# Rotary attention: probabilities times values as three fp16 passes, and slots of TensorE, VectorE and ScalarE in another order

## The reference

```python
def _L3_attn_ref(x, w_qkv, w_out):          # H = 16 heads, D = 128
    qkv = jnp.einsum('bsd,od->bso', x, w_qkv).reshape(B, S, 3 * H, D)
    q, k, v = qkv[:, :, :H, :], qkv[:, :, H:2 * H, :], qkv[:, :, 2 * H:, :]
    cos, sin = _rope_tables(S, D, x.dtype)
    q = _apply_rope(q, cos, sin)            # x * cos + rotate_half(x) * sin
    k = _apply_rope(k, cos, sin)
    logits = jnp.einsum('bqhd,bkhd->bhqk', q, k) / math.sqrt(D)
    attn = jax.nn.softmax(logits.astype(jnp.float32), axis=-1)
    out = jnp.einsum('bhqk,bkhd->bqhd', attn, v).reshape(B, S, H * D)
    return jnp.einsum('bso,do->bsd', out, w_out)
x = x + _L3_attn_ref(_layernorm(x), L3_attn_w_qkv, L3_attn_w_out)
```

## Time and profile before

| | before |
|---|---|
| median of 3 runs | 3325.28 us (3325.05 to 3331.84) |
| the profiled execution | 3327.55 us, its span 3325.8 us |
| mean granted TensorE clock | 0.941 of full |
| PE busy | 2894.7 us (87%), 25209 instructions |
| PEld busy | 2207.1 us (66%) |
| DVE busy | 2245.0 us (68%), 5436 instructions |
| ACT busy | 1854.3 us (56%) |
| POOL busy | 1732.8 us (52%) |
| DMA | 102.31 MB, mean 31 GB/s |
| l3a: first projection to last output projection | 2087.2 to 2587.2 us |

### The profile page before, as it was taken

The page is one execution under the profiler, slowest core; times in us unless marked ns, Lnnn a source line. Parts: engine busy times, 40 slices in busy tenths (PEclk is TensorE's granted clock), DMA queues, the critical chain, the costliest instruction groups (busy, mean ns, idle before and its releaser), DMA issues. The chain is left out here.

```text
span 3325.8 us, 71661 instructions
## 1 busy us (share of the span) xinstructions
PE 2894.7 (87%) x25209; PEld 2207.1 (66%) x25209; DVE 2245.0 (68%) x5436; ACT 1854.3 (56%) x3544; POOL 1732.8 (52%) x1835
## 2 busy tenths in 40 slices
PE   7969989788999774895777999899999799998898
PEld 5747765457778453563555555788888688886565
DVE  5567755756777703885886677566665677777787
ACT  3357753446666221563665565566666577775575
POOL 2122211314555365564773466788888588886132
PEclk9979999799999875897999999999999999999899
DMA  4010010000000343000001531000000000000001
GB/s 158 1 23 14 13 69 1 7 5 8 7 6 3 111 120 85 5 6 24 15 16 66 204 89 48 3 0 0 0 0 1 7 7 5 5 5 13 16 25 38
DMA packets 93886, 102.31 MB, mean 31 GB/s; under 512 B 41500, under 2 KB 80860, under 8 KB 90719
## 3 DMA queue, kind: packets, MB, share of 16 engines
q1 hardware_dynamic: 89064, 93.98, 9.2%
q0 software_dynamic: 4608, 5.57, 1.0%
HBM read 80.84 MB, written 11.61 MB: 28 GB/s over the span
## 5 line engine op out<-in xcount | busy, mean ns | idle before, releaser
L1905 PE MATMUL bank<-l3a_ln_xnT,far 128*128 128x128 f16 x3072 | 184.5, 221 | 1.8 <-POOL l3a_ln_xnT L1721 1.8
L1905 PEld LDWEIGHTS bank<-l3a_ln_xnT,far 128*128 128x128 f16 x3072 | 179.6, 99 | 3.4 <-POOL l3a_ln_xnT L1721 2.2
L877 PE MATMUL bank<-l2f_xnT,l2f_wi 128*128 128x512 f16 x672 | 156.6, 382 | 7.0 <-POOLq L741 6.4
L388 DVE SCALAR_TENSOR_TENSOR x_res<-bank,l3f_combine,x_res 128x256 f32<-128x256 f32 x320 | 132.8, 478 | 26.3 <-PE bank L541 24.1
L3185 PE MATMUL bank<-l0x_v,l0x_pT 128*128 128x128 f32 x1024 | 134.0, 279 | 3.2 <-ACT l0x_pT L3612 1.5
L3185 PEld LDWEIGHTS bank<-l0x_v,l0x_pT 128*128 128x128 f32 x1024 | 127.0, 192 | 13.8 <-issue 4.7
L2789 POOL TENSOR_TENSOR l1x_prob<-l1x_prob,l1x_srec 128x512 f32<-128x512 f32 x64 | 67.8, 1059 | 121.5 <-DVE l1x_srec L2560 121.5
L541 PE MATMUL bank<-l3f_wd,l3f_h 128*128 128x256 f16 x960 | 119.4, 275 | 12.9 <-DVE l3f_h L380 12.9
L541 PEld LDWEIGHTS bank<-l3f_wd,l3f_h 128*128 128x128 f16 x960 | 94.5, 99 | 42.0 <-DVE l3f_h L380 13.6
L531 PE MATMUL bank<-l3f_xnT,l3f_wi 128*128 128x512 f16 x480 | 119.2, 386 | 0.4 <-issue 0.4
L2701 ACT ACTIVATE l3x_prob<-bank,l3x_less,l3x_q_rr 128x128 f32<-128x128 f32 x256 | 96.5, 457 | 37.1 <-DVE l3x_less L2583 37.0
(11 more groups left out here) (727 smaller groups left out, 9416.9 us busy)
## 6 DMA issues: line engine op xcount, KB each, us to landing
far<-in_l1f_in SPq DMA_DIRECT2D x32, 256.0 KB, 3.9
l2f_front<-l2f_shares SPq DMA_DIRECT2D x5, 1024.0 KB, 5.0
sums<-near SPq DMA_DIRECT2D x2, 2176.0 KB, 19.2
far<-in_l1f_down SPq DMA_DIRECT2D x32, 128.0 KB, 4.1
l1f_xn<-sums SPq DMA_DIRECT2D x32, 128.0 KB, 2.3
l2f_wi<-in_l2f_in SPq DMA_DIRECT2D x14, 256.0 KB, 5.9
far<-l0x_kT SPq DMA_DIRECT2D x64, 48.0 KB
far<-l2x_kT SPq DMA_DIRECT2D x32, 96.0 KB, 2.5
```

Source lines behind the costliest of these rows:

```text
L388: last = nc.vector.scalar_tensor_tensor(core.x[:, b, :], y, combine[:, b, bass.ds(n, 1)], core.x[:, b, :], ALU.mult, ALU.add)
L877: last = nc.tensor.matmul(bank[:, :], wi16[n % 2][p][:, a, k, :], xnT[q][:, k, 512 * g:512 * g + 512], start=(k + p + q == 0), stop=(k == ...
L1905: last = nc.tensor.matmul(bank[:, P * j:P * j + P], w(k, 512 * c + P * j, P, p), norm.xnT[u][q][:, k, :], start=(k + p + q == 0), stop=(k ...
```

## The change

The probabilities and the values are now kept as fp16 halves. `keep_probs` and `keep_v` on ScalarE write the high halves (same number of operations, fp16 out), two new functions on VectorE write the low halves: `low_probs` (L2020 of the changed kernel) from b_p, `low_values` (L2025) from b_v, each with a wait of its own on a new semaphore (`pT_hi`, `v_hi`). The semaphores on which TensorE waits, `pT_kept` and `v_kept`, are now set by VectorE. `heads_out` issues 12 fp16 matmuls in place of four fp32 ones. The orders within `slot` change on TensorE, VectorE and ScalarE; the code of GpSimd is the same. The tiles take the same room in SBUF. Cut to its core:

```diff
-        v = [sb(f"v{c}", [P, KC * P]) for c in range(NC)]
+        v = [[sb(f"v{c}{i}", [P, KC * P], F16) for i in range(2)] for c in range(NC)]
-        pT = sb("pT", [P, 512])
+        pT = [sb(f"pT{i}", [P, 512], F16) for i in range(2)]
+        pT_hi, v_hi = sem("pT_hi"), sem("v_hi")
...
                     for j in range(HC):
                         at = P * (j * KC // HC)
-                        last = nc.tensor.matmul(b_o[:, P * j:P * j + P], v[c][:, at:at + P],
-                                                pT[:, P * j:P * j + P], start=True, stop=True)
+                        for p, q in HALVES:
+                            last = nc.tensor.matmul(b_o[:, P * j:P * j + P], v[c][p][:, at:at + P],
+                                                    pT[q][:, P * j:P * j + P], start=(p + q == 0), stop=(p == 1))
...
                     if pr:
                         turn_probs(pr)
-                    if ou:
-                        project_out(ou)
...
-                    if pr:
-                        heads_out(pr)
...
                     if proj:
                         project_q(proj)
+                    if ou:
+                        project_out(ou)
+                    if pr:
+                        heads_out(pr)
+                    if proj:
                         project_k(proj)
...
+                def low_probs(it):
+                    b, u, c, f = it
+                    dve.wait_ge(pT_hi, f + 1)
+                    nc.vector.tensor_tensor(pT[1][:, :], b_p[:, :], pT[0][:, :], ALU.subtract).then_inc(pT_kept, 1)
+
+                def low_values(it):
+                    b, u, c, f = it
+                    dve.wait_ge(v_hi, f + 1)
+                    nc.vector.scalar_tensor_tensor(v[c][1][:, :], b_v[:, 0:KC * P], 1.0 / W_SCALE, v[c][0][:, :],
+                                                   ALU.mult, ALU.subtract).then_inc(v_kept, 1)
...
+                    if sc:
+                        low_values(sc)
+                    if pr:
+                        low_probs(pr)
+                    if proj and prep == "rope":
+                        rotate(q_made, b_q, qa, q_parts, qT_kept, proj)
+                    if ex:
+                        sums(ex)
                     if ou and ou[2] == NC - 1:
                         residual(ou)
-                    if ex:
-                        sums(ex)
                     if pr:
                         keep_o(pr)
                     if proj and prep == "rope":
-                        rotate(q_made, b_q, qa, q_parts, qT_kept, proj)
                         rotate(k_made, b_k, ka, k_parts, kT_kept, proj)
...
-                    nc.scalar.copy(pT[:, :], b_p[:, :]).then_inc(pT_kept, 1)
+                    nc.scalar.copy(pT[0][:, :], b_p[:, :]).then_inc(pT_hi, 1)
...
-                        nc.scalar.activation(v[c][:, :], b_v[:, 0:KC * P], ACT.Copy, scale=1.0 / W_SCALE
-                                             ).then_inc(v_kept, 1)
+                        nc.scalar.activation(v[c][0][:, :], b_v[:, 0:KC * P], ACT.Copy, scale=1.0 / W_SCALE
+                                             ).then_inc(v_hi, 1)
...
-                    if pr:
-                        keep_o(pr)
...
                     if proj and prep == "rope":
                         swap(proj, q_parts, b_q, qb, qT_kept, q_swapped)
+                    if pr:
+                        keep_o(pr)
+                    if proj and prep == "rope":
                         swap(proj, k_parts, b_k, kb, kT_kept, k_swapped)
```

More of the change, by code:

```diff
@@ L2132, in keep_v @@
                             act.wait_ge(mask_set, b + 1)
-                        nc.scalar.activation(v[c][:, :], b_v[:, 0:KC * P], ACT.Copy,
-                                             scale=mcol_b[u][:, 0:1]).then_inc(v_kept, 1)
-                    else:
-                        nc.scalar.activation(v[c][:, :], b_v[:, 0:KC * P], ACT.Copy, scale=1.0 / W_SCALE
-                                             ).then_inc(v_kept, 1)
+                        nc.scalar.activation(v[c][0][:, :], b_v[:, 0:KC * P], ACT.Copy,
+                                             scale=mcol_b[u][:, 0:1]).then_inc(v_hi, 1)
+                    else:
+                        nc.scalar.activation(v[c][0][:, :], b_v[:, 0:KC * P], ACT.Copy, scale=1.0 / W_SCALE
+                                             ).then_inc(v_hi, 1)
                 def exponentials(it):
```

## The result

| | before | changed |
|---|---|---|
| median | 3325.05 us (5 runs) | 3307.86 us (3303.97 to 3310.11, 5 runs) |
| the profiled execution | 3327.55 us, span 3325.8 | 3306.64 us, span 3304.9 |
| l3a, from its first norm transposes to those of l3x | 509.0 us | 491.5 us |

What follows compares the result with a forecast made beforehand. TensorE's issue was taken to bound l3a; -12.4 (product) + 0.5 (waits) - 1.5 (first slot) - 1.0 (end) = -14.4 us, from 3327.55 to 3313.2, so a median of 3311 us. Range 3306.6 to 3321.

Steps and rivals of the forecast that it cites:

- What bounds: In l3a's loop TensorE, busy 100.00, sets the time; edits elsewhere cost nothing until they make it wait.
- Part 1: Heads' sums: 12 fp16 matmuls replace four fp32 ones, saving 0.207 us a slot, 12.4 us over 60 slots.
- The range's upper term: Largest saving counted for the product in heads' sums: 15.3 us in the range's sum, beside 0.25 us a slot.
- The 81 ns rule: Skill's pace for sustained load and matmul pairs: heads' sums would take 0.97 us, losing 0.08 us a slot.
- Part 2: Two more VectorE operations a slot, 0.692 us each, end 0.8 us before heads' sums in most slots.
- The 0.5 us booked for waits: Total TensorE waiting in 14 slots that begin with the normalisation, where the low half has no slack; bounds 0 and 4.5.
- the ring: Not forecast: ScalarE and VectorE chain between successive slots' low halves, without TensorE operations, about 7.1 us a slot.
- Rival A: GpSimd holds both new VectorE operations, TensorE waits 0.6 us a slot: +24 us, kernel at 3349; chance 4%.
- B: Heads' sums' 98 ns weight loads do not overlap: +17.5 us over 60 slots, kernel at 3340; chance 3%.
- C: VectorE's new chain ends around 3.4 us into every slot, TensorE gives back its 0.2, kernel at 3323; chance 10%.
- Part 3: Query work moves ahead on TensorE, VectorE and ScalarE, covering the probabilities' low half; cost zero inside the loop.
- The ends: First slot with probabilities saves 1.5 us, bounds 0 and 2.3; the layer's last slots save 1.0 us.

Runs made afterwards that it cites:

- the run with 0.6 us more on the ring: Low half of the probabilities computed twice, against the changed kernel: l3a 516.8 us against 491.5, mean slot 7.737 us against 7.379.
- the orders alone: New orders of TensorE, VectorE and ScalarE with the fp32 product kept, against the kernel before: ratio 0.9992, l3a 504.4 us.
- the cheap product alone: fp16 product with its two new VectorE operations but all old orders, against the kernel before: median 3362.83 us, ratio 1.0105, l3a 543.6 us.
- TensorE's order alone: The change with TensorE's new order but VectorE's and ScalarE's orders as before, against the kernel before: ratio 1.0004, l3a 508.6 us.

## Why the prediction came out as it did

**What bounds: right.** TensorE at 100.00 in the loop before and after, no wait of it between 2111 and 2552 us.

**Part 1, the product: right in kind, 7% short.** Forecast 0.207 a slot, measured 0.223. The pair was taken at 0.0569 us from 48 of them over 2.73 us of weight-load starts; by matmul starts it is 0.0558, and the old group 0.90 and not 0.89. On 60 slots that is 1 us. The range's upper term, 15.3, is not what the prediction works out for it (60 x 0.25 = 15.0); with 15.0 the lower edge would be 3306.9. The 81 ns rule of the Trainium skill (TensorE: Matmul & The Clock Gate, Back-to-back issue gap) that was weighed there does not hold for this stream, also with 24 pairs in the group. The same section gives a single matmul's spacing as N/2.4 + 2.5 ns, 55.8 for 128 columns; that one the runs agree with.

**Part 2, VectorE in time: right for the kernel as it is, its reason half right.** The 0.5 us booked for waits stays unspent: the normalisation, laid out at 1.37 us, takes 0.41 in the loop. And the slack that I read off one slot was no price list: the ring was there in the same layout, and I did not follow it round. Rival A's mechanism did not occur (0.680 and 0.692 in all slots), nor B's. C did not either, but the run with 0.6 us more on the ring shows how close it stood: 0.24 us a slot in the mean.

**Part 3, the reordering as cover at no cost: right.** The loop of the orders alone is unchanged; without them the product costs 0.52 a slot, where I had put 0.5 before the saving.

**The ends: the term that failed.** The step that failed is the size of the first slot's term. I took 1.5 us; it gave 3.5. I kept the copy's time of the old trace, although the same edit lets ScalarE's swaps go earlier (1.2: the copy came 1.59 us behind the transposes and not 2.81), and of my own layout's 1.6 to 2.3 I took less than the least, where TensorE stayed at the 2.4 GHz level and the upper value applied. At the end I took 1.0; the orders gave 1.2, and the product with its low half took 0.6 of it back: 0.6.

Together: -13.4 in place of -12.4 + 0.5, -3.5 in place of -1.5, -0.6 in place of -1.0, so -17.5 in place of -14.4.

## What to carry to other kernels

Four fp32 matmuls of 128x128 cost 0.89 us here, and the 12 fp16 passes that replace them 0.67. But the low halves' latency has to be put behind work that does not need them; measure the product and its cover apart, since here the cheap product alone lost 35 us. Before trusting a slack in one slot of a software pipeline, follow the chain round to the same operation of the next slot: it can close without touching the busiest engine, and then the difference between its length and the busiest engine's slot is what new work may take. The first slots of a pipeline are a chain of their own, and a changed order can move them.

## What the hardware showed

A VectorE operation can be three times as long for the moment at which it starts. The normalisation (fp32, SBUF to SBUF) ends 0.15 to 0.2 us after the GpSimd operation that was running. Begun 0.05 after this one's start it took 1.37 (2306.46, in the earlier trace rows), and begun 0.2 before its end 0.41; first the kernel before, then the changed one:

```profile
2306.41 1.27 POOL L2207 TENSOR_TENSOR l3a_qT<-l3a_qa,l3a_qb 128x512 f32<-128x512 f32 x1 [0.20 <-issue]
...
2322.82 1.26 POOL L2227 TENSOR_TENSOR l3a_qT<-l3a_qa,l3a_qb 128x512 f32<-128x512 f32 x1 [0.20 <-issue]
...
2323.85 0.41 DVE L1693 TENSOR_SCALAR l3a_ln_xn<-x_res,l3a_ln_mv,l3a_ln_rstd 128x256 f32 x1
```

The Trainium skill (SBUF — State Buffer, Who interferes with whom) has VectorE and GpSimd exclude each other on a shared port pair, and names this kind of operation; the median of the same line, 1372 ns before, 1078 with the orders alone, 704 with TensorE's order alone and 405 after, fits it. It does not show that the operation stands still all the while: it ends 0.15 us behind GpSimd's, and alone it takes 0.40, as in l3x.

A longer loop body came with standstills of TensorE. With the fp16 group doubled, six rounds of l3a's loop began with up to 2.9 us without a cause in the semaphores. The page's queue of instruction transfers, of the changed kernel and of that one:

```profile
q8 instruction: 122, 2.00, 0.3%
```

```profile
q8 instruction: 178, 2.92, 0.4%
```

That is 56 more transfers of code. They lie in the loop: from 2170 to 2520 us the doubled kernel has 46 of them and the changed one none, and three fall between 2185 and 2191, around the standstill that ends at 2190.17. The doubled fp32 product (123) has neither the transfers nor the standstills. That the transfers are TensorE's code, fetched again in each round because the body of eight slots has grown, is the likely cause and was not tried by itself, nor from what size on it happens.
